# A four-layer kernel on one Trainium2 core: the third layer's statistics and first normalised rows made in the second layer's last tile, its weights in five DMAs, a part of the fourth's statistics in the third

## The reference, cut to what matters

```python
def _layernorm(x, axis=-1, eps=1e-05):
    m = jnp.mean(x, axis=axis, keepdims=True)
    v = jnp.var(x, axis=axis, keepdims=True)
    return (x - m) / jnp.sqrt(v + eps)
...
    x = x + s * g
    xn = _layernorm(x, axis=-1)
    s = _L2_attn_ref(xn, L2_attn_Wq, L2_attn_bq, L2_attn_Wk, L2_attn_bk, L2_attn_Wv, L2_attn_bv, L2_attn_Wo, L2_attn_bo)
    g = _silu(_L2_ffn_ref(xn, L2_ffn_w_gate, L2_ffn_w_up, L2_ffn_w_down))
    x = x + s * g
```

## Time and profile before

| | us |
|---|---|
| median of 3 executions | 4652.23 |
| lowest and highest | 4651.94, 4652.31 |
| the profiled execution | 4657.47 |
| its span, first to last instruction | 4655.7 |
| PE busy in it | 4411.0 (95%) |
| DVE busy | 2495.7 (54%) |
| ACT busy | 1688.0 (36%) |

### The profile page before, as it was taken

One profiled execution on the slowest core, in us unless ns is written; L12 is line 12 of the kernel. 1 busy time (PEld: TensorE's weight loads), 2 busy tenths in 40 slices (PEclk: granted clock), 3 DMA queues, 4 the chain that ended last, 5 costly groups with the idle time before them and its releaser, 6 DMA issues. The chain is left out here.

```text
span 4655.7 us, 56266 instructions
## 1 busy us (share of the span) xinstructions
PE 4411.0 (95%) x19733; PEld 2576.7 (55%) x19733; DVE 2495.7 (54%) x5806; ACT 1688.0 (36%) x3238; POOL 202.5 (4%) x324
## 2 busy tenths in 40 slices
PE   7999989999999999999999997999997896999997
PEld 3444446756666675666667664666665443333332
DVE  6666653242524334252433415886987776666664
ACT  2444442232322323232232323444442221455554
POOL 0122200000000000000000000000000000000000
PEclk8999999999999999999999998999998998999999
DMA  2011012112121211212121111000000000101011
GB/s 81 16 18 35 16 46 73 73 66 79 55 78 67 73 73 68 77 64 82 55 91 64 65 63 42 0 1 0 1 1 18 0 1 19 20 15 17 15 20 40
DMA packets 50467, 196.47 MB, mean 42 GB/s; under 512 B 9592, under 2 KB 19200, under 8 KB 32904
## 3 DMA queue, kind: packets, MB, share of 16 engines
q1 hardware_dynamic: 49392, 192.84, 12.6%
q10 hardware_dynamic: 816, 0.20, 0.0%
HBM read 169.54 MB, written 4.33 MB: 37 GB/s over the span
## 5 line engine op out<-in xcount | busy, mean ns | idle before, releaser
L1077 PE MATMUL l_exp_out<-l_w,l_hidden 128*128 128x256 f32 x4096 | 905.2, 381 | 0.3
L1067 PE MATMUL l_hid<-l_xn_t,l_w 128*128 128x512 f32 x2048 | 891.1, 593 | 0.0
L1077 PEld LDWEIGHTS l_exp_out<-l_w,l_hidden 128*128 128x128 f32 x4096 | 774.1, 190 | 118.8 <-issue 9.0
L1191 ACT ACTIVATE l_hidden<-l_hid,l_w 128x512 f32<-128x512 f32 x512 | 351.4, 686 | 930.2 <-PE l_hid L1067 930.2
L1067 PEld LDWEIGHTS l_hid<-l_xn_t,l_w 128*128 128x128 f32 x2048 | 388.9, 190 | 466.4 <-issue 453.6
L446 DVE TENSOR_REDUCE l3f_row_max<-l3f_bank 128x1 f32<-128x512 f32 x512 | 327.6, 684 | 187.9 <-PE l3f_bank L329 187.5
L1344 DVE SCALAR_TENSOR_TENSOR l_moe<-l_exp_out,l_gates,l_moe 128x256 f32<-128x256 f32 x256 | 123.5, 483 | 451.7 <-PE l_exp_out L1077 446.0
L402 ACT ACTIVATE l3f_prob_t<-l3f_bank 128x512 f32<-128x512 f32 x512 | 278.1, 595 | 226.3 <-PE l3f_bank L336 226.1
L336 PE MATMUL l3f_bank<-l3f_qk_t 32*128 32x512 f32 x1024 | 312.5, 637 | 2.9 <-ACT l3f_prob_t L402 2.5
L443 DVE CUSTOM_DVE_ANT_0 l_masked<-l_bank,l_mask 128x256 f32<-128x256 f32 (+3 forms) x512 | 226.7, 487 | 161.3 <-PE l_bank L329 160.5
L329 PE MATMUL l3f_bank<-l3f_qk_t 32*128 32x512 f32 x1024 | 298.7, 646 | 8.3 <-DMA l3f_qk_t<-l3f_set_rows 8.0
(11 more groups left out here) (444 smaller groups left out, 6095.3 us busy)
## 6 DMA issues: line engine op xcount, KB each, us to landing
l_w<-in_w SPq DMA_DIRECT2D x128, 1024.0 KB, 4.9
l_mix<-l_cum SPq DMA_DIRECT2D x32, 512.0 KB, 3.7
l_qk_t<-l_packed SPq DMA_DIRECT2D x128, 64.0 KB
l3f_qk_t<-l3f_packed SPq DMA_DIRECT2D x128, 64.0 KB
all_x<-in_x SPq DMA_DIRECT2D x8, 512.0 KB, 6.5
out_x<-all_x SPq DMA_DIRECT2D x8, 512.0 KB, 5.7
l_hidden<-in_fp4w SPq DMA_DIRECT2D x1, 2304.0 KB
l_qk_t<-l_max_rows SPq DMA_DIRECT2D x128, 2.0 KB
```

What stands on the lines that cost most here:

```text
L1067: ins = nc.tensor.matmul(bank[:, :], w1[:, e % 2, c, f * P:(f + 1) * P], xn_t[:, c, :], start=c == 0, stop=c == CT - 1)
L1077: ins = nc.tensor.matmul(bank[:, 0:C], hidden[:, e % 2, f, j * P:(j + 1) * P], w2[:, e % 2, f, :], start=f == 0, stop=f == HF - 1)
L1191: hid.empty(nc.scalar.activation(hidden[:, e % 2, f, :], bank[:, :], ACT.Relu, bias=w[:, B1][:, e * HF + f:e * HF + f + 1]), (e, f))
```

## The change

One object, `Norms`, now lives beside x for the whole program: `xn`, the statistics, means, roots and inverses of all tiles, and two semaphores. Every layer uses its buffers.

- In the second layer's last tile DVE makes statistics of tiles 0 to 6 after expert 4, ACT takes their roots, and DVE makes their inverses and tile 0's normalised rows after expert 5.
- The SiLU, the product and the addition to x at that tile's end are done in four parts, each when its expert sum is there.
- The third layer loads q's weights, the biases, k's, v's and o's in five DMAs with a semaphore each, then the FP4 weights. PE's first transposes wait for no data. ACT copies them first, then splits the first FP4 weight; the second is split after q and k. DVE normalises tile 1 first, and makes the statistics of tile 7 alone.
- At the third layer's end 16 of the fourth's 32 statistics (tiles 0 to 3) are made before the last gate; the fourth makes four for each row group instead of eight.

```diff
+class Norms:
+    def __init__(self, a):
+        self.xn = a.sb("xn", [P, TJ, C])
+        self.stats, self.meanvar = a.sb("stats", [P, B, TJ, 6]), a.sb("meanvar", [P, B, TJ, 2])
+        self.var_eps, self.std, self.rstd = (a.sb(n, [P, B, TJ]) for n in ("var_eps", "std", "rstd"))
+        self.early_var, self.early_std = a.sem("early_var"), a.sem("early_std")
+
+    def partial(self, nc, x_all, b, j):
+        return nc.vector.bn_stats(self.stats[:, b, j, :], x_all[:, b, j, :])
...
 def layer1
...
+                    if e == 5 and is_last:
+                        act.wait_ge(norms.early_var, 1)
+                        norms.roots(nc, slice(0, B - 1)).then_inc(norms.early_std, 1)
...
+                if is_last:
+                    for j in range(TJ):
+                        exp_out.wait_emptied(act, b, (E - 1, j))
+                        nc.scalar.activation(moe[:, j, :], moe[:, j, :], ACT.Silu).then_inc(gate_ready, 1)
...
+                def gated(j):
+                    jobs.wait_emptied(dve, b, f"o{j}")
+                    dve.wait_ge(gate_ready, b + j + 1)
+                    st.link(V.tensor_tensor(s[:, j, :], s[:, j, :], moe[:, j, :], ALU.mult))
+                    st.link(V.tensor_tensor(x_all[:, b, j, :], x_all[:, b, j, :], s[:, j, :], ALU.add))
...
+                            if e == E - 1 and j:
+                                gated(j - 1)
...
+                    if e == 4 and is_last:
+                        norms.variances(nc, st, x_all, range(0, B - 1)).then_inc(norms.early_var, 1)
+                    if e == 5 and is_last:
+                        dve.wait_ge(norms.early_std, 1)
+                        st.link(norms.inverses(nc, slice(0, B - 1)))
+                        norms.tile(nc, x_all, 0)
...
 def layer2
...
-            sp.dma_start(w[:, 0:WO.start], w_dram[:, 0:WO.start]).then_inc(w_loaded, 16)
-            sp.dma_start(w[:, WO.start:], w_dram[:, WO.start:]).then_inc(w_loaded, 16)
+            sp.dma_start(w[:, WQ], w_dram[:, WQ]).then_inc(q_loaded, 16)
+            sp.dma_start(w[:, BQ.start:], w_dram[:, BQ.start:]).then_inc(bias_loaded, 16)
+            sp.dma_start(w[:, WK], w_dram[:, WK]).then_inc(k_loaded, 16)
+            sp.dma_start(w[:, WV], w_dram[:, WV]).then_inc(v_loaded, 16)
+            sp.dma_start(w[:, WO], w_dram[:, WO]).then_inc(o_loaded, 16)
...
             def normal_in(t):
-                pe.wait_ge(xn_ready, t + 1)
+                if t:
+                    pe.wait_ge(xn_ready, t)
...
-            pe.wait_ge(w_loaded, 32)
             normal_in(0)
             query_key(0)
+            pe.wait_ge(v_loaded, 16)
             value(0)
...
-            roots(1, slice(0, FIRST))
+            normal_in(0)
             act.wait_ge(fp4_loaded, 16)
-            for k in range(2):
-                fh.split(weight(k), weight(k), weight_lo(k))
-            normal_in(0)
-            act.wait_ge(w_loaded, 32)
+            fh.split(weight(0), weight(0), weight_lo(0))
+            act.wait_ge(bias_loaded, 16)
             query_key(0, 0)
+            fh.split(weight(1), weight(1), weight_lo(1))
             value(0)
...
             flow.start_empty(dve)
-            variances(range(0, FIRST))
-            inverses(1, slice(0, FIRST))
-            normalise(0)
+            normalise(1)
             normalise_again(0)
-            dve.wait_ge(w_loaded, 32)
+            norms.variances(nc, st, x_all, range(LAST, B)).then_inc(var_ready, 1)
+            dve.wait_ge(bias_loaded, 16)
             start_weight(0)
-            normalise(1)
...
             finish_weight(0)
-            variances(range(FIRST, B))
             start_weight(1)
...
             quantise_rows(LAST, 3)
+            for b in range(HALF):
+                for j in range(TJ):
+                    norms.partial(nc, x_all, b, j)
             gated(LAST)
...
 def layer3_positions
...
-                for b in range(B):
-                    ins = V.bn_stats(stats[:, b, :], x_all[:, b, j, :])
+                for b in range(HALF, B):
+                    ins = norms.partial(nc, x_all, b, j)
...
 def build
...
+        norms = Norms(a)
```

More of the change, by code:

```diff
@@ L139, in by_tile, with variances, roots, inverses @@
     return ap.rearrange("p (j q) -> p j q", q=P)
+class Norms:
[6 more added lines that the diff above has]
+        return nc.vector.bn_stats(self.stats[:, b, j, :], x_all[:, b, j, :])
+    def variances(self, nc, st, x_all, tiles):
+        for b in tiles:
+            for j in range(TJ):
+                ins = self.partial(nc, x_all, b, j)
+        st.link(ins)
+        for b in tiles:
+            for j in range(TJ):
+                ins = nc.vector.bn_aggr(self.meanvar[:, b, j, :], self.stats[:, b, j, :])
+        st.link(ins)
+        span = slice(tiles[0], tiles[-1] + 1)
+        return nc.vector.tensor_scalar(self.var_eps[:, span, :], self.meanvar[:, span, :, 1], LN_EPS, None, ALU.add)
+    def roots(self, nc, tiles):
+        return nc.scalar.activation(self.std[:, tiles, :], self.var_eps[:, tiles, :], ACT.Sqrt)
+    def inverses(self, nc, tiles):
+        return nc.vector.reciprocal(self.rstd[:, tiles, :], self.std[:, tiles, :])
+    def tile(self, nc, x_all, b):
+        for j in range(TJ):
+            ins = nc.vector.tensor_scalar(self.xn[:, j, :], x_all[:, b, j, :], self.meanvar[:, b, j, 0:1], self.rstd[:, b, j:j + 1],
+                                          ALU.subtract, ALU.mult)
+        return ins
 class LayerNorm:
     LINKS = 3
-    def __init__(self, a, n_tiles):
+    def __init__(self, a, n_tiles, xn=None):
         self.n = n_tiles
@@ L1609, in query_key @@
                     flow.wait_emptied(pe, ("xt", t, c))
-                for name, wx in (("q", wq), ("k", wk)):
+                for name, wx, loaded in (("q", wq, q_loaded), ("k", wk, k_loaded)):
+                    if not t:
+                        pe.wait_ge(loaded, 16)
                     for f in range(DT_):
```

100 lines of the change are left out of this document (42 added, 58 removed).

## The result

Over nine runs each, the changed kernel takes 4642.0 us (4638.9 to 4644.4), the kernel before 4654.9 us (4650.8 to 4661.2): ratio 0.9973, with a 95% interval of 0.9963 to 0.9983. So the change makes the kernel faster, by 12.9 us of medians or 0.3%. Forecast were 4636.8 us and a gain of 15.4 us, with a range up to 4641.2 us. The direction holds, the time lies 0.8 us beyond the range. Of the 5.2 us between forecast and median, 2.7 us lie in the base: the three runs from which the forecast started had a median of 4652.2, the nine have 4654.9. The other 2.5 us are gain that did not come.

The account below looks back on a forecast made before the run. PE, busy in 95% of the span, was taken as the bound, the layer following when PE is first fed without a break. 16.5 - 1.7 + 1.35 - 0.8 = 15.4 us off 4652.2 gave 4636.8 us, range 4633.5 to 4641.2.

Parts of the forecast that it names:

- The second layer's last tile: 28 statistics and aggregations added on DVE, 11.5 us, hide in its 14.98 us wait, 3.5 us left: cost nothing.
- Its end: End of the second layer: SiLU in four pieces lets the last addition end 3.1 us earlier, at most 3.8.
- The third layer's start: First scores start at 2853.9 instead of 2870.39, set by DVE behind the FP4 weights: 16.5 us earlier, 3.1 us included.
- the rival's 8.4 us: Third layer's loads: each small DMA pays its own start, FP4 weights 8.4 us later, 4645.2 us in all; chance 0.06.
- The clock behind the new hole: Third layer: PE stands still from about 2850.3 to 2853.9, and the clock's fall behind it loses 1.7 us.
- The third layer from tile 1 on: PE's later groups should find their data ready, so the 16.5 us at the first scores is guarded.
- the rivals: Chances: no clock fall 0.18; second hold, larger fall or late issue 0.24; more gain 0.07; full DMA starts 0.06; slower 0.01.
- The prediction's own sign of being wrong: FP4 landing later than 14.1 us after first issue, PE waiting in the second tile, or first-scores gain missing at layer's end.
- 24 statistics off DVE: Third layer: 24 statistics with aggregations (7.93 + 1.70 + 0.18 us) leave DVE between the two weights; gives nothing more.
- The fourth layer: Four of the first eight statistics go, so PE's first transposes gain 1.35 us; 16 statistics moved earlier cost nothing.
- The end: Program's end: two outermost semaphores, cleared with one more barrier of all engines behind the output, add 0.8 us.
- The base: Starting point of the forecast: the kernel before at a median of 4652.2 us, from which 15.4 us was taken.

## Why the prediction was right, and where it was wrong

- **The second layer's last tile**: right. The 28 statistics are hidden with 3.6 us to spare (forecast 3.5).
- **Its end**: right, 3.3 us for 3.1; the instructions took 0.41 to 0.43 us each, not 0.48.
- **The third layer's start**: nearly right, 16.2 us for 16.5, with DVE behind the FP4 weights as the last chain, as worked out. What was off is "I take the same landing": it came 14.8 us behind the first issue, not 14.05, so the sentence "The rate doesn't follow the number of DMAs if the queue is never empty" is short by some 0.6 us for three more DMAs. That is far from the rival's 8.4 us. By the 2 us of fixed cost that the Trainium skill (DMA: Bandwidth & Descriptors, Anatomy of one DMA) gives for a DMA issued by GpSimd, three more would have cost 6 us, an estimate; for these, which SP issues, the traces show a tenth of it.
- **The clock behind the new hole**: right, 8.80 to 10.60 us is 1.8 us for the 1.7 us forecast. The cause of the hole was named too, and yet the sum took it as given; to put features first was there to be seen in the earlier trace rows.
- **The third layer from tile 1 on**: this is the step that failed. The prediction says that "PE's later groups should find their data ready", and they do; no wait is added. It took from this that the gain stays. The clock doesn't follow waits alone: PE was busy through the row sums, 20 columns in 2.29 us, and behind them two more groups than before had 3.4 us at half clock, 1.7 us lost in each. That is 3.4 of the 3.8 us that went; with the spells gone from both kernels 3.0 us came back. None of the rivals had this. The prediction's own sign of being wrong, a gain at the first scores that is not there at the layer's end, did appear; PE's wait in the second tile did not. The Trainium skill (TensorE: Matmul & The Clock Gate, Why this matters for your kernels) asks for no long idle gap between bursts of matmuls; here the profile shows no gap at all, and the clock falls. In the earlier trace rows PE stands at 1.00 from 2870 to 3000; the slow groups of the kernel before lie behind that stretch, from tile 5 on, where I did not look.
- **24 statistics off DVE**: right, worth nothing.
- **The fourth layer**: the direct part is right (1.3 us), but the term is 3.2 to 3.4 us: 1.0 us comes from PE's half clock at the layer's start, which ends 3.3 us sooner, and 0.9 us from shorter half-clock stretches in three later groups. The prediction priced the clock behind the new hole and not behind these old ones. That this unforeseen gain made up for nearly half of the 4.2 us that went in the third layer is luck.
- **The end**: 0.4 us for 0.8.
- **The base**: three runs stood for a median; E alone moves by several us, so 2.7 us of the miss were in the starting point, and the range left no room for it.

## What to carry to other kernels

A wait that is taken away moves all that follows, and where the clock's spells hang on the moment, the same work then takes another time: compare two traces from a common mark, group by group, before a remainder is put down to the change, and look for small matmuls that keep TensorE busy with one column each (to widen them cost 0.05 us for 20 here and took 6.5 us off the layer). Where an engine is fed earlier, look at who comes last now: five DMAs in place of two lost 2.3 us in the one order of ACT and DVE and gained 2.9 us in the other.

## What I had not expected of the hardware

TensorE lost its full clock while the profile shows it busy all the time: behind 2.29 us of one-column products the granted clock was at half for 3.4 us, in five tiles of the layer or in two, as 1 us of delay came in (three in the kernel before, four with two DMAs, none with 64 columns). A tile that was hit took 85.25 us, where an undisturbed one takes 83.57 us, and from tile 3 on the next was hit again in every trace; behind tile 1, hit in three traces, tile 2 never was. What a moment must have to be hit I can only describe by these cases. And eight semaphores more at the outermost level cost next to nothing (16.0 for 15.9 us at the end, in one execution).
